# First attention layer: turning attention rows and row maxima with VectorE in 32x32 blocks, and dividing on GpSimd

## The reference

```python
x = x + _layernorm(_L0_attn_ref(_layernorm(x, axis=-1), w_qkv, b_qkv, w_o, b_o), axis=-1)
# _L0_attn_ref: b=16 sequences, l=256 tokens, h=16 heads, c=8
qkv = jnp.einsum('bld,ed->ble', x, w_qkv) + b_qkv            # split in q, k, v, heads of 8
attn = jax.nn.softmax(jnp.einsum('blhc,bmhc->bhlm', q, k) * SCALE, axis=-1)
heads = jnp.einsum('bhlm,bmhc->blhc', attn, v).reshape(b, l, d)
return jnp.einsum('bld,ed->ble', heads, w_o) + b_o + x
```

## Time and profile before

| | |
|---|---|
| median of 3 runs | 689.94 us (689.15 to 693.46) |
| the profiled execution: its own time | 688.81 us |
| its span, first to last instruction | 686.9 us |
| busy: PE, DVE, ACT, POOL | 579.7, 428.4, 376.1, 326.0 us |
| first layer | from 0 to about 372 us |
| one iteration of its loop | about 20.0 us |

### The profile page before, as it was taken

One profiled execution on the slowest core, in us unless ns is written; L12 is line 12 of the kernel. 1 busy time (PEld: TensorE's weight loads), 2 busy tenths in 40 slices (PEclk: granted clock), 3 DMA queues, 4 the chain that ended last, 5 costly groups with the idle time before them and its releaser, 6 DMA issues. The chain is left out here.

```text
span 686.9 us, 16311 instructions
## 1 busy us (share of the span) xinstructions
PE 579.7 (84%) x5450; PEld 434.8 (63%) x5450; DVE 428.4 (62%) x1221; ACT 376.1 (55%) x989; POOL 326.0 (47%) x542
## 2 busy tenths in 40 slices
PE   4899999999999999999983688889888408999930
PEld 3555666666666666666652577778777407999920
DVE  2455566666766666666622478888776643788870
ACT  1114655656565565656571399886775005677650
POOL 5320142343235565531213545775887860257776
PEclk9999999999999999999996599998887557999985
DMA  5000423000000000000011000000000022234333
GB/s 151 17 2 2 156 63 50 8 20 17 18 19 17 19 5 16 17 18 17 18 31 34 30 2 1 3 1 2 10 20 26 35 86 62 53 43 68 41 30 31
DMA packets 32658, 21.63 MB, mean 31 GB/s; under 512 B 7609, under 2 KB 30913, under 8 KB 32578
## 3 DMA queue, kind: packets, MB, share of 16 engines
q1 hardware_dynamic: 15072, 10.65, 6.5%
q0 software_dynamic: 6640, 4.92, 5.1%
q10 hardware_dynamic: 10866, 5.03, 2.8%
HBM read 10.11 MB, written 8.12 MB: 27 GB/s over the span
## 5 line engine op out<-in xcount | busy, mean ns | idle before, releaser
L385 DVE TENSOR_REDUCE nmax<-psA 128x2 f32<-128x512 f32 x256 | 165.2, 688 | 121.5 <-PE psA L208 121.2
L513 ACT ACTIVATE pr<-psB 128x512 f32<-128x512 f32 x250 | 135.9, 595 | 123.8 <-PE psB L225 123.1
L208 PE MATMUL psA<-km,q 24*128 24x256 f32 x768 | 139.9, 428 | 3.4 <-POOL km L611 2.1
L208 PEld LDWEIGHTS psA<-km,q 24*128 24x128 f32 x768 | 91.8, 198 | 29.3 <-issue 17.5
L225 PE MATMUL psB<-q,km 26*128 26x256 f32 (+1 forms) x752 | 109.9, 411 | 0.0
L1626 POOL DMA_INDIRECT out<-wz,ys x39 | 63.5, 1627 | 53.4 <-ACT wz L1581 44.5
L611 POOL TENSOR_TENSOR km<-kraw,rows_of 128x768 f32<-128x768 f32 x16 | 23.5, 1467 | 118.7 <-DVEq L364 114.5
L239 PE MATMUL psO<-pr,v 128*32 128x256 f32 x1024 | 69.4, 389 | 1.3 <-ACT osb L507 1.1
L225 PEld LDWEIGHTS psB<-q,km 26*128 26x128 f32 (+1 forms) x752 | 69.0, 190 | 0.2 <-issue 0.2
L585 POOL TENSOR_SCALAR ve<-mv_r 128x2 f32<-128x2 f32 x16 | 3.8, 236 | 105.9 <-DVE mv_r L346 105.9
L1189 ACT ACTIVATE prob<-psS,nbias 128x128 f32<-128x128 f32 x128 | 45.6, 382 | 10.8 <-DVE nbias L1008 10.8
(11 more groups left out here) (199 smaller groups left out, 1241.2 us busy)
## 6 DMA issues: line engine op xcount, KB each, us to landing
ys<-y_sorted SPq DMA_DIRECT2D x39, 72.0 KB, 1.9
e_w<-W ACTq DMA_DIRECT2D x1, 2048.0 KB
e_w<-W ACTq DMA_DIRECT2D x4, 512.0 KB
xs<-x_all SPq DMA_DIRECT2D x16, 128.0 KB
out<-x_all SPq DMA_DIRECT2D x15, 128.0 KB, 3.7
x_all<-x SPq DMA_DIRECT2D x1, 1536.0 KB, 10.6
q<-mT SPq DMA_DIRECT2D x64, 4.0 KB
out<-wz,ys POOLq DMA_INDIRECT x39, 3.4
```

The lines of the kernel that those rows point to most:

```text
L208: last = T.matmul(psA[:, n % 2, c * L1:(c + 1) * L1], queries(b, h, depth, slice(c * P, (c + 1) * P)), keys(b, h, depth, slice(0, L1)), st ...
L385: V.tensor_reduce(nmax[:, b % 2, :, h], psA[:, n % 2, :].rearrange("p (c m) -> p c m", c=2), AX.X, ALU.max, negate=True).then_inc(S["a_fre ...
L513: A.activation(pr[:, h % PRING, :, :].rearrange("p c l -> p (c l)"), bank_of(b, h), ACT.Exp, scale=SCALE1).then_inc(S["b_free"], 1)
```

## The change

- The maxima: `nmax` now has its two halves of 128 queries in one block of 32 columns, DVE turns it in 32x32 blocks (`turn_maxima`) straight to `mT`, and SP sends each head's row with a DMA of its own, 8 in a half batch in place of 2. PE's transposes and ACT's copy go.
- The attention rows: DVE turns the whole of `psO` (128x512) in 32x32 blocks to `oT` (`turn_rows`). PE's `heads_to_tokens` and ACT's copy go.
- The division: GpSimd raises the 128x16 denominators to the power -1 and multiplies (`normalise`), before `spread` in its iteration. DVE's reciprocal and multiplication go.
- The way back: DVE turns `on` (128x256) in blocks (`heads`), ACT adds the bias; `heads_T` goes. `project` is for batch i - 1 in group 7, in place of batch i - 2 in group 2, and PE's and ACT's loops are one iteration shorter.
- Blocks of 32 leave tokens in an order of their own, so the queries for the maxima are written a second time by ACT in that order (`qp`, two more activations for each batch), and w_o and the value bias are loaded with their heads reordered: w_o in 4 DMAs in place of 1, the value bias in 4 DMAs that PE's bias step waits for.

```diff
-        for i in range(LAST + 3):
-            for what, b in ((("tokens", 0), i - 1), (("xT",), i + 2), (("max", 1), i), (("out",), i - 2),
-                            (("v",), i + 1), (("q",), i + 2), (("tokens", 1), i - 1), (("max", 0), i + 1),
-                            (("k",), i + 2), (("heads",), i - 1)):
...
+        for i in range(LAST + 2):
+            for what, b in (("xT", i + 2), ("v", i + 1), ("q", i + 2), ("k", i + 2), ("out", i - 1)):
...
-            pe.wait_ge(S["ld_b"], 128)
+            pe.wait_ge(S["ld_b"], 192)
...
+            last = T.matmul(misc[bank][:, 4:5], bv_row[0:1, :], one[:, :],
+                            start=True, stop=True)
...
                 for c in range(2):
                     last = T.matmul(psA[:, n % 2, c * L1:(c + 1) * L1],
-                                    queries(b, h, depth, slice(c * P, (c + 1) * P)),
+                                    query_part(b, h, depth, c),
                                     keys(b, h, depth, slice(0, L1)), start=True, stop=True)
...
-                    if g == 0 and done:
-                        heads_to_tokens(i - 1, 0)
                     if g == 0 and fits(i, 2):
                         prep_x(i + 2)
                     if g == 1 and done:
                         attend(i - 1, 3)
-                    if g == 1 and here:
-                        max_rows(i, 1)
-                    if g == 2 and fits(i, -2):
-                        project(i - 2)
...
-                    if g == 4 and done:
-                        heads_to_tokens(i - 1, 1)
-                    if g == 5 and next_:
-                        max_rows(i + 1, 0)
...
                     if g == 7 and done:
-                        heads_T(i - 1)
+                        project(i - 1)
...
+            def turn_maxima(b, hf):
+
+                dve.wait_ge(S["a_free"], 16 * b + HALF * hf + HALF)
+                dve.wait_ge(S[f"mrow{hf}"], 16 * HALF * b)
+                V.transpose(mT[:, hf, :],
+                            nmax[:, b % 2, hf, :, :].rearrange("p c h -> p (c h)")).then_inc(S["turned"], 1)
+
+            def turn_rows(b, hf):
+
+                dve.wait_ge(S["av_done"], 4 * b + 2 * hf + 2)
+                dve.wait_ge(S["norm_ok"], count(2 * (b - 1) + hf + 1))
+                V.transpose(oT[:, hf, :, :, :].rearrange("p a m r -> p (a m r)"), psO[:, :]).then_inc(S["o_ev"], 1)
+
+            def heads(b):
+
+                dve.wait_ge(S["norm_ok"], 2 * b + 2)
+                dve.wait_ge(S["onT_ok"], b)
+                V.transpose(onR[:, :], on[:, :, :, :].rearrange("p m a e -> p (m a e)")).then_inc(S["heads_ok"], 1)
 
             def iteration(i):
                 next_, done = fits(i, 1), fits(i, -1)
                 for g in range(8):
+                    if g == 2 and done:
+                        turn_rows(i - 1, 1)
+                    if g == 6 and fits(i, 0):
+                        turn_rows(i, 0)
                     if next_:
                         maxima(i + 1, 2 * g)
                         maxima(i + 1, 2 * g + 1)
-                    if g == 0 and done:
-                        normalise(i - 1, 0)
-                    if g == 1 and fits(i, EARLY):
+                    if g in (3, 7) and next_:
+                        turn_maxima(i + 1, g // 4)
+                    if g == 0 and fits(i, -2):
+                        residual(i - 2)
+                    if g == 1 and fits(i, -2):
+                        residual_stats(i - 2)
+                    if g == 5 and done:
+                        heads(i - 1)
+                    if g == 4 and fits(i, EARLY):
                         stats_x(i + EARLY)
...
-                act.wait_ge(S["q_ok"], 2 * b + 2)
+                act.wait_ge(S["a_full"], count(16 * (b - 1)))
+                for t in range(2):
+                    A.activation(qp[:, b % 2, t, :].rearrange("p (c k r) -> p k c r", c=2, r=32),
+                                 misc[bank][:, t * L1:(t + 1) * L1].rearrange("p (k c r) -> p k c r", c=2, r=32),
+                                 ACT.Identity, bias=b_cols[:, t:t + 1]).then_inc(S["q_ok"], 1)
...
-            act.dma_start(w_nat[:, 3, :], w_o).then_inc(S["ld_wo"], 16)
+            for a in range(4):
+                act.dma_start(w_nat[:, 3, :].rearrange("p (j a c) -> p a j c", a=4, c=C1)[:, a, :, :],
+                              w_o.rearrange("p (a j c) -> p a j c", j=4, c=C1)[:, a, :, :]).then_inc(S["ld_wo"], 16)
...
+            def normalise(b, hf):
+                pool.wait_ge(S["o_ev"], 2 * b + hf + 1)
+                pool.wait_ge(S["norm_ok"], 2 * b + hf)
+                if hf == 0:
+                    pool.wait_ge(S["heads_ok"], b)
+                G.tensor_tensor(rden[:, :, :], oT[:, hf, :, :, C1], minus_one[:, :, :], ALU.pow
+                                ).then_inc(S["rden_ok"], 1)
+                pool.wait_ge(S["rden_ok"], 2 * b + hf + 1)
+                G.tensor_tensor(out=on[:, :, 2 * hf:2 * hf + 2, :].rearrange("p m a e -> p a m e"),
+                                in0=oT[:, hf, :, :, 0:C1],
+                                in1=rden[:, :, :].unsqueeze(3).broadcast_to([P, 2, 8, C1]),
+                                op=ALU.mult).then_inc(S["norm_ok"], 1)
+
             def iteration(i):
...
                 if fits(i, -2):
                     add_attention(i - 2)
+                if fits(i, -1):
+                    normalise(i - 1, 1)
+                if fits(i, 0):
+                    normalise(i, 0)
                 if fits(i, 2):
                     spread(i + 2)
...
-                for k in range(2):
-                    tile, row = ((0, 24), (0, 25), (0, 26), (1, 24))[2 * hf + k]
-                    sp.dma_start(q[row:P:32, b % SLOTS, tile, :],
-                                 mT[4 * k:4 * k + 4, hf, :]).then_inc(S[f"mrow{hf}"], 16)
+                for at in range(HALF):
+                    tile, row = ((0, 24), (0, 25), (0, 26), (1, 24))[2 * hf + at // 4]
+                    row += 32 * (at % 4)
+                    sp.dma_start(q[row:row + 1, b % SLOTS, tile, :], mT[at:P:16, hf, :]).then_inc(S[f"mrow{hf}"], 16)
...
+            for a in range(4):
+                sp.dma_start(bv_row[:, :].rearrange("o (j a c) -> o a j c", a=4, c=C1)[:, a, :, :],
+                             by_head[:, a, :, :]).then_inc(S["ld_b"], 16)
             load_x(2)
-            sp.dma_start(bv_col[:, :], b_qkv[2 * P:3 * P].rearrange("(p o) -> p o", o=1),
-                         allow_slow_non_contiguous=True).then_inc(S["ld_v"], 16)
```

138 lines of the change are left out of this document (44 added, 94 removed).

## The result

The changed kernel takes 705.8 us (median of four runs, 703.7 to 711.1) where the kernel before took 689.6 in the same job (689.2 to 693.5): 1.023 times as long, interval 1.016 to 1.031. The forecast was 690.5 with a range of 684 to 706, so the time stands at the very edge of the range, 0.2 us inside it and 15 from the forecast itself, and it is the rival "exposed power" that came. The profiled execution took 707.7 us, its span 705.9, which is 19.0 more than the 686.9 of before.

A forecast was written before the change was run, and what follows sets the result against it. The bound was PE's first-layer loop, chained with DVE's reductions in pairs of groups plus tails behind `attend`. Loop -3.75, start +2.9 and end +1.7 gave +0.85 on 688.81, so 689.7, or 690.5 us as a median; range 684 to 706.

The forecast's parts named there:

- exposed power: Rival, slower: GpSimd's power beyond 2.3 us makes `spread` late each iteration; 710.7 us at 3.2; chance 0.28.
- The chain of a pair of groups: First layer's loop: each pair takes 4.60 us plus the odd group's tail; even tails free under about 1.2; iteration 20.01 to 19.67.
- DVE's turns: DVE in groups 2 and 6: turns of 0.70 and 0.42 us fit, with cover of 0.05 and 0.2.
- exposed turns: Rival, slower: a 128x512 turn of 1.38 us delays reductions of groups 2 and 6; iteration 20.8, 706 us; chance 0.10.
- The power: GpSimd's division of 128x16: between 0.73 and 3.2 us, taken half and half as 1.96.
- the forecast's own case: GpSimd's power from 0.73 to 2.3 us gives 687 to 697 us in all; chance 0.52.
- From P to the period: P, the power's time, precedes `spread`: PE opens at 17.8 + P if later than 19.67; with 1.96, iteration 19.76, gain 0.25.
- GpSimd's other customers: DVE's `heads` waits for GpSimd's division, done by 11, or 4.3 later with expert biases; late only from 14.3 plus 0.2.
- ACT and SP: ACT, busy 55%, is off the chain; SP's 8 sends take 4 us a half, hidden with about 4 us to spare.
- The start: Lead-in: four more bias loads on SP (2.7) and one more PE product (0.4), taken as +2.9 us, unhidden.
- The end: First layer's last batch: `normalise(15, 1)` behind `add_attention(14)`; finish at 371.65 + P, 373.6 with P of 1.96, or +1.7 us.
- The sum: Whole kernel: -3.75 + 2.9 + 1.7 = +0.85 us on 688.81, giving 689.7, or 690.5 as a median.

The follow-up runs named there:

- The experiment with `heads_T`: The kernel before with only the maxima part of the change, and `heads_T` moved from group 7's tail to group 6's: 680.6 us, ratio 0.989.
- the halves: The changed kernel with each power of 128x16 split into two of 128x8: 741.5 us, ratio 1.050.
- the reordered version: The changed kernel with GpSimd doing `spread(i + 2)` ahead of `normalise(i, 0)`: 697.7 us, ratio 1.014.
- the maxima alone: The kernel before with only the maxima part of the change and its second set of queries: 681.0 us, ratio 0.986.
- the second profile of before: The kernel before, unchanged, profiled a second time: 693.4 us.
- the second pair of profiles: The changed kernel and the kernel before, each profiled a second time without edits: 707.5 and 693.4 us.

## Why the prediction went as it did

**The chain of a pair of groups**: right. `attend` starts 2.43 after DVE's reductions of the even group in the changed kernel too (191.16 and 193.59 above). Tails behind `attend` count and those of even groups do not, within bounds: 19.67 was forecast for the loop without a hindrance, and 19.65 is what it takes with the power gone. The experiment with `heads_T` shows the bound, about 1.2 us for an even tail, that the prediction stated: with `prep_qk` and two transposes in it the tail of group 6 was 1.24, and the expectation for that run put it at 1.28, over its own bound of 1.2, and yet counted the whole gain.

**DVE's turns**: right. 0.709 and 0.434 us for 0.70 and 0.42, and they hide: the reductions of group 6 wait 0.31 for PE behind the turn, for a forecast cover of 0.2. The Trainium skill, "VectorE: DVE Perf Modes", section on the three transpose paths, gave by its figure of 311 ns for 128x128 bf16 an estimate near 0.7. The prediction does not say how it came from 128 columns to 512 (four times the figure would be 1.24), but the trace bears the estimate out: by 0.211 us for 32 columns and 0.434 for 256 a turn has a fixed part of 0.18 us and 0.001 for each column, which would be 0.31 at 128 columns and 0.69 at 512, and 0.709 was measured. The rival "exposed turns" is out.

**The power**: this is the step that failed. The two bounds were 0.73 and 3.2 and the value taken halfway between, 1.96; measured 2.91. With it the forecast's own case (a power of up to 2.3, slack for `spread` used up but no more) fell, and the gain of 0.25 an iteration became a loss of 0.38. The upper bound, all of the excess by element, was 0.3 too high only because the fixed part of a power, 0.40, is a little more than the 0.354 of other work; the mechanism behind it was right, and the halves with 1.643 show it. "Half and half" had no row for it: one row of two elements can't say more, as the prediction said, but then the case in which two elements already cost 0.36 us extra deserved more than 0.28. The Trainium skill, "GPSIMD Engine Reference", section 3, would have had 1.06 for the division and multiplication by its ratio for `tensor_tensor` (an estimate); the trace has 3.32, so that ratio, which the page gives for an addition, does not hold for a power.

**From P to the period**: the place was right (P beyond 1.87 makes `spread` late), the sum 0.3 too long. 17.8 + 2.91 is 20.7, measured 20.39, since the power starts at 15.3 in the iteration, not 15.5 (190.93 less 175.61), and the multiplication takes 0.41, not 0.54 to 0.6.

**GpSimd's other customers**: `heads` waits for nothing in the changed kernel, as forecast. It is the reordered version that runs into it.

**ACT and SP**: right, hidden. SP's eight sends take 4.8 us, for 4.

**The start**: right up to the bias step. It started 2.5 later (10.54 for 8.07) and is one product longer, and PE's first product for the maxima came 2.9 later, as forecast. These are the rows:

```profile
6.86 2.42 SPq L716 DMA_DIRECT2D bv_row<-b_qkv  x4
...
10.54 1.83 PE L170 MATMUL misc<-one,brow 1*128 1x1 f32 x8 [3.46 <-DMA bv_row<-b_qkv]
12.24 0.56 PE L172 MATMUL misc<-one,bv_row 1*128 1x1 f32 x2
...
21.73 1.14 PE L215 MATMUL psA<-km,qp 24*128 24x256 f32 x8 [1.49 <-POOL km L583]
```

PE's first product for the maxima is at 21.73 (18.82 before), and yet the first `attend` is only 1.8 later. The prediction left out that the change also shortens the lead-in: the maxima alone reach the first `attend` 1.1 earlier than before (0.6 by the second profile of before).

**The end**: right in its structure, with a slip in its sum. `add_attention(14)` stands in the way from 377.17 to 380.19, 3.02 long. From the last `attend` to the last `x_all` the forecast had 371.65 + P - 360.2, so 14.4 with the measured P, and it is 14.70. Its terms add up to more than it says, though: 364.4 + 0.75 + 0.5 + 0.55 + 1.7 + 4.27 is 372.17, so the 0.5 of the turn was left out, and the rightly added sum has 14.9. The gain of 1.3 ahead of it came as 0.8; the short fall of the clock at 361 to 366 us lies in that stretch (without it, in the version with the reciprocal on DVE, the stretch takes 22.13 for 23.72, a gain of 1.6).

**The sum**: with P = 2.91 the prediction's own working gives 15 x 0.70 + 2.9 + 2.6 = +16.0 on 689.9, so 706 as a median, and 705.8 was measured. That agreement is partly luck. (The forecast of 690.5 is itself 0.3 short of its terms: 688.81 + 0.85 + 1.1 is 690.8.) The loop took 0.38 an iteration and not 0.70, the start 1.8 and not 2.9 (2.3 between the second pair of profiles, 58.55 and 56.24); falls of PE's clock, which the prediction named as a way to be wrong and gave no price, made up for the difference. About 4 us of the 16.1 are left for them when the period, start, end and the second layer's 0.8 are taken off (the 0.8 by which two executions of the kernel before differ there too): 16.1 - 15 x 0.38 - 1.8 - 3.5 - 0.8 = 4.3. That the time fell inside the range at all is luck of the same kind: by 0.2 us, at its slow end, while the forecast itself missed by 15.

**What stays open**: what the clock follows. Extra work filled idle stretches and raised PE's busy share at once, and no run parts the two. The share of a long stretch does not order all the cases (93.5% without a fall, 94.7% with one); the number, the length and the place of the idle stretches are not separated.

## What to carry to other kernels

Before an operation is moved to another engine, its price there has to be measured at its size, or the forecast made with the bound that counts every element: here the power took 0.157 us for each column, where ordinary work took 0.00145, and a batch of reciprocals belonged on the engine that does them in 0.25 us. Take a change that bundles several moves apart: one part (the maxima) held the gain, another (the division) most of the loss. And an idle time of 5% on TensorE need not be free, even where nothing waits for TensorE: count it in the risk.
